# The attention stage of a vision tower on Trainium2, taken in pairs of tiles, with outputs token by token

## The reference

```python
x    = layernorm(h)
q, k = elu(x @ Wq) + 1, elu(x @ Wk) + 1          # per head, 64 channels
v    = x @ Wv
A    = (q @ k.T) * causal                         # 37 x 37, per image and head
out  = (A @ v) / max(A.sum(-1), 1e-6)
h    = h + sigmoid(x @ Wg) * (out.reshape(-1, 256) @ Wo)
```

## Time and profile before

| | |
|---|---|
| Runs (median of 3) | 1119.67 us (1112.85 to 1121.09) |
| The profiled execution's own time | 1121.94 us |
| Its span, first to last instruction | 1120.0 us |
| Mean granted clock of TensorE | 0.840 of 2.4 GHz |
| PE busy | 951.7 us (85%) |
| DVE busy | 528.6 us (47%) |

### The profile page before, as it was taken

One profiled execution on the slowest core, in us unless ns is written; L12 is line 12 of the kernel. 1 busy time (PEld: TensorE's weight loads), 2 busy tenths in 40 slices (PEclk: granted clock), 3 DMA queues, 4 the chain that ended last, 5 costly groups with the idle time before them and its releaser, 6 DMA issues.

```text
span 1120.0 us, 18357 instructions
## 1 busy us (share of the span) xinstructions
PE 951.7 (85%) x5804; PEld 664.2 (59%) x5804; DVE 528.6 (47%) x1712; ACT 323.8 (29%) x908; POOL 312.6 (28%) x308
## 2 busy tenths in 40 slices
PE   6667999968999998887769899996575999999990
PEld 5555777746664555554545467774563777777670
DVE  5983678864443232222753368864672222222210
ACT  1332233323343322222122256662201222222210
POOL 3881000000000000000042045541017277677444
PEclk9995899975557999999975579996556999999995
DMA  8778000000002999995350000000205244544222
GB/s 253 218 271 346 1 0 0 0 1 1 1 1 80 419 423 422 422 424 215 104 141 1 0 1 2 0 2 8 60 3 140 53 83 82 83 80 74 35 22 21
DMA packets 64187, 125.82 MB, mean 112 GB/s; under 512 B 26910, under 2 KB 47184, under 8 KB 54912
## 3 DMA queue, kind: packets, MB, share of 16 engines
q1 hardware_dynamic: 34176, 115.69, 28.8%
q0 software_dynamic: 29952, 9.36, 6.4%
HBM read 112.83 MB, written 11.98 MB: 111 GB/s over the span
## 4 chain that ended last, share of the span: by engine, by line
PE 67%; DMA 12%; DVE 9%; issue 6%; POOL 2%; ACT 2%; SPq 1%; DVEq 0%; POOLq 0%; ACTq 0%
PE bank L1747 14%; DMA ys<-eo 10%; PE bank L1757 6%; PE bank L738 4%; PE bank L743 3%; PE bank L1432 3%; PE bank L909 2%; PE bank L1518 2%; PE bank L1048 2%; PE bank L927 2%; PE bank L1442 2%; PE bank L1458 2%; PE bank L774 1%; PE bank L907 1%; PE bank L925 1%
## 5 line engine op out<-in xcount | busy, mean ns | idle before, releaser
L1747 PE MATMUL bank<-zT,w 96*128 96x372 f32 x512 | 161.8, 477 | 0.0
L1156 POOL MEMSET xg<- 96x74 f32 x1 | 0.2, 157 | 478.0 <-PE bank L1130 478.0
L1747 PEld LDWEIGHTS bank<-zT,w 96*128 96x128 f32 x512 | 97.4, 191 | 61.0 <-issue 0.5
L1692 POOL DMA_INDIRECT out_dram<-yr,put x48 | 105.7, 2203 | 90.0 <-issue 62.0
L1803 DVE TENSOR_TENSOR hT<-sg,bank 128x372 f32<-128x372 f32 x64 | 34.7, 542 | 126.4 <-PE bank L1747 126.4
L1678 POOL DMA_INDIRECT zr<-z_rows,take x48 | 66.5, 1385 | 85.4 <-issue 83.9
L990 DVE COPY eh<-bank 128x384 f32<-128x384 f32 x32 | 17.8, 558 | 119.4 <-PE bank L1026 119.4
L1048 PE MATMUL bank<-w2s,eg 128*64 128x192 f32 x768 | 69.4, 330 | 0.0
L1776 ACT ACTIVATE sg<-bank 128x372 f32<-128x372 f32 x64 | 30.7, 480 | 128.0 <-PE bank L1747 128.0
L715 PE MATMUL bank<-wtok_g,xT 128*111 128x192 f32 x264 | 47.9, 332 | 20.9 <-DVE y L628 20.9
L1757 PE MATMUL bank<-w2r,hT 128*124 128x192 f32 x384 | 63.7, 326 | 0.0
(11 more groups left out here) (277 smaller groups left out, 1801.0 us busy)
## 6 DMA issues: line engine op xcount, KB each, us to landing
w1s<-in_w_dram SPq DMA_DIRECT2D x32, 1152.0 KB, 12.6
w2s<-in_w_dram SPq DMA_DIRECT2D x32, 1152.0 KB, 14.7
xt<-in_x_dram SPq DMA_DIRECT2D x22, 336.0 KB, 3.9
xT<-in_xT_dram SPq DMA_DIRECT2D x22, 333.0 KB, 3.6
w<-in_w_dram SPq DMA_DIRECT2D x8, 768.0 KB
ys<-eo SPq DMA_DIRECT2D x64, 48.0 KB, 9.3
w2r<-in_w2r_dram SPq DMA_DIRECT2D x8, 384.0 KB
e<-ys SPq DMA_DIRECT2D x21, 96.0 KB, 2.0
```

Of the source, the lines that this page charges most:

```text
L1692: nc.gpsimd.indirect_dma_start(rows_out, bass.IndirectOffsetOnAxis(ap=put[:, k:k + 1], axis=0), yr[e % 2][:, j, :], None, bounds_check=OUT ...
L1747: last = nc.tensor.matmul(bank[2 + 2 * (m % 2) + part][:, 0:HS], w13[b][:, c, at:at + 128], zT[b][:, c, half * HS:(half + 1) * HS], start= ...
```

## The change

The attention stage is taken in 11 pairs of tiles, 222 tokens (`PAIR`), and each engine's program is written out in full, without the loop:

- `products_qk` moves the 222 tokens of a pair against the same 128 columns of weights: eight matmuls a pair instead of sixteen. `products_vg` is as before, twice, and is a step of its own.
- `scores`, `project` and `transpose_h` have the same matmuls, those of two tiles in one step.
- `values` holds the masked scores of a head (111 columns) and moves `vx`, which has 64 channels and a 65th column of ones: the product comes out token by token, and its 65th column is the denominator. The matmuls with ones are gone, and so is the use of half the array's columns.
- `normalize_out` bounds and inverts 4 numbers a token instead of 222 columns, and multiplies into `on`. `transpose_o` turns `on` by four transposes a pair, and ACT copies them to `oT` (`copy_oT`).
- All of `fe`, `fr`, `qk`, `vx`, `am`, `on`, `oT` and `rg` have one buffer; `ha`, `haT` and `gate` have two. Bank 7 holds, in turn, the first tile's values, the turned outputs and the projection; bank 0 the transposed input and the second tile's values.

Its core:

```diff
-                for j in range(4):
-                    for c in range(2):
-                        last = nc.tensor.matmul(bank[1][:, j * TP:(j + 1) * TP], wqk[:, c, j * 128:(j + 1) * 128], hnT[b][:, c, :], start=(c == 0), stop=(c == 1))
+                for j in range(4):
+                    for c in range(2):
+                        last = nc.tensor.matmul(bank[1 + j // 2][:, j % 2 * PAIR:(j % 2 + 1) * PAIR], wqk[:, c, j * 128:(j + 1) * 128], x[:, c, :], start=(c == 0), stop=(c == 1))
...
-                for j in range(2):
-                    for r in range(2):
-                        half = slice(64 * r, 64 * r + 64)
-                        nc.tensor.matmul(bank[5][half, j * TP:(j + 1) * TP], vx[b][:, 2 * j + r, :], am[b][:, 2 * r + j, :], start=True, stop=True)
-                for r in range(2):
-                    last = nc.tensor.matmul(bank[6][64 * r:64 * r + 64, 0:2 * TP], ones[0:TP, 0:64], am[b][:, 2 * r:2 * r + 2, :].rearrange("p j q -> p (j q)"), start=True, stop=True)
+                for i in range(2):
+                    for n in range(NH):
+                        last = nc.tensor.matmul(bank[0 if i else 7][0:TP, n * (DH + 1):(n + 1) * (DH + 1)], am[:, n % 2, i, n // 2, :], vx[:, i, n, :], start=True, stop=True)
                 last.then_inc(s_bav, 1)
...
+            def transpose_o(p):
+                pe.wait_ge(s_bon, p + 1)
+                flat = on[:].rearrange("p i h d -> p i (h d)")
+                for i in range(2):
+                    for j in range(2):
+                        last = nc.tensor.transpose(bank[7][:, (2 * i + j) * TP:(2 * i + j + 1) * TP], flat[:, i, j * 128:(j + 1) * 128], ident[0:TP, 0:TP])
+                last.then_inc(s_bt, 1)
+
+            for p in range(T // 2 + 2):
+                if p < T // 2:
+                    transpose_h(p)
+                if 1 <= p <= T // 2:
+                    scores(p - 1)
+                if p >= 2:
+                    project(p - 2)
+                if p < T // 2:
+                    products_qk(p)
+                if 1 <= p <= T // 2:
+                    values(p - 1)
+                if p < T // 2:
+                    products_vg(p)
+                if 1 <= p <= T // 2:
+                    transpose_o(p - 1)
...
+            def normalize_out(p):
+
+                dve.wait_ge(s_bav, p + 1)
+                if p:
+                    dve.wait_ge(s_bt, p)
+                out = [bank[b][0:TP, 0:NH * (DH + 1)].rearrange("p (h d) -> p h d", h=NH) for b in (7, 0)]
+                for i in range(2):
+                    last = nc.vector.tensor_scalar(den[:, i, :], out[i][:, :, DH], 1e-6, None, ALU.max)
+                last.then_inc(s_bd, 1)
+                dve.wait_ge(s_bd, 2 * p + 1)
+                nc.vector.reciprocal(rden[:], den[:]).then_inc(s_bd, 1)
+                dve.wait_ge(s_bd, 2 * p + 2)
+                for i in range(2):
+                    last = nc.vector.tensor_tensor(on[:, i], out[i][:, :, 0:DH], rden[:, i, :].unsqueeze(2).to_broadcast([TP, NH, DH]), ALU.mult)
+                last.then_inc(s_bon, 1)
```

More of the change, by code:

```diff
@@ L448, in tower @@
         s_bwo = sem("attn_projected")
+        s_bt = sem("attn_out_transposed")
+        s_bo = sem("attn_oT_copied")
         s_brg = sem("attn_gated")
@@ L538, in attention_act @@
             h_std(act, 0)
[L540 to L562, removed]
+            def copy_hT(p):
+                act.wait_ge(s_hTr, 2 * p + 2)
+                if p >= 2:
+                    act.wait_ge(s_bvg, p - 1)
+                nc.scalar.copy(haT[p % 2][:], bank[0][0:HALF, 0:2 * PAIR].rearrange("p (c q) -> p c q", c=2)).then_inc(s_hTc, 2)
@@ L564, in embed_act, with copy_oT @@
+            def copy_oT(p):
+                act.wait_ge(s_bt, p + 1)
+                if p:
+                    act.wait_ge(s_bwo, p)
+                nc.scalar.copy(oT[:], bank[7][:, 0:4 * TP].rearrange("p (i j q) -> p i j q", i=2, j=2)).then_inc(s_bo, 1)
+            for p in range(T // 2 + 1):
+                if p < T // 2:
+                    copy_hT(p)
+                    features(p)
+                    values(p)
+                if p:
+                    copy_oT(p - 1)
         def embed_act(act):
@@ L669, in mask @@
[L669 to L674, removed]
-                last.then_inc(s_bam, 1)
[L677 to L686, removed]
@@ L731, in products, with scores @@
[L731 to L735, removed]
+                    for i in range(2):
+                        last = nc.tensor.transpose(bank[0][0:HALF, c * PAIR + i * TP:c * PAIR + (i + 1) * TP], ha[p % 2][:, i, c * HALF:(c + 1) * HALF], ident[0:TP, 0:TP])
+                last.then_inc(s_hTr, 2)
+            def scores(p):
+                pe.wait_ge(s_bq, p + 1)
+                if p:
+                    pe.wait_ge(s_bam, p)
+                for i in range(2):
+                    at = slice(i * TP, (i + 1) * TP)
+                    for j in range(2):
+                        for r in range(2):
+                            rows = slice(64 * r, 64 * r + 64)
+                            last = nc.tensor.matmul(bank[5 + r][0:TP, (2 * i + j) * TP:(2 * i + j + 1) * TP], qk[rows, 2 + j, at], qk[rows, j, at], start=True, stop=True)
+                last.then_inc(s_bs, 1)
@@ new lines, in project, with products_qk @@
+            def project(p):
+                pe.wait_ge(s_bo, p + 1)
+                for i in range(2):
+                    for j in range(2):
+                        last = nc.tensor.matmul(bank[7][0:TP, i * ED:(i + 1) * ED], oT[:, i, j, :], wo[:, j, :], start=(j == 0), stop=(j == 1))
+                last.then_inc(s_bwo, 1)
+            def products_qk(p):
+                pe.wait_ge(s_hTc, 2 * p + 2)
+                if p:
+                    pe.wait_ge(s_bf, p)
+                x = haT[p % 2]
```

151 lines of the change are left out of this document (91 added, 60 removed).

## The result

The changed kernel takes 1100.77 us (median of 4 runs, 1098.82 to 1102.81), against 1119.33 for the kernel before, measured anew beside it (4 runs, 1112.85 to 1121.09): a ratio of 0.9845 with a 95% interval of 0.980 to 0.989, 18.6 us less. The profiled execution took 1102.81 us, with a span of 1101.0, 19.0 shorter than before.

A forecast was written before the change was run, and what follows sets the result against it. TensorE's queue was taken to bound the attention stage: -11.3 us of its work, +1.5 of stall and -7.4 from the clock made -17.2, so 1104.7 for the profiled execution and 1103 predicted, range 1094 to 1115.

The forecast's parts named there:

- q and k: Attention's q/k product: 3.74 us a pair become 16 records of 222 columns, 2.99, plus one exposed weight load: -0.65.
- scores: Attention scores: changing to half the rows and back happens once a pair of tiles, 0.95 us a pair, -0.2.
- projection: Attention's output projection: eight records at 0.162 us, 1.30 a pair, as the change to half the columns goes: -0.19.
- inputs: Input transposes of attention: four at 0.093 us and one start of 0.1, 0.47 a pair: -0.19.
- values: Attention values and denominators: 1.82 us a pair become 16 records, taken as 1.55: -0.27, bounds -0.95 and +0.05.
- outputs turned: New output transposes in attention: four a pair with 128 columns held, +0.47 us, bounds 0.37 and 0.66.
- The stall: PE waiting on the ACT and DVE chain in attention: 0.15 us a pair for ten pairs, +1.5, bounds 0 and +5.
- The clock: At attention's beginning the clock rises by about 104 us instead of 120: -7.4 us, bounds 0 and 9.
- The late rise (1): Rival: the clock in the attention stage rises no sooner than before, 1110 us; chance 0.15.
- a chain that binds (2): Rival: attention's single-buffered chain over ACT and DVE becomes the bound, ten pairs lose 8 us, 1111; chance 0.13.
- The third: Rival: attention's clock stays low well beyond 120 us; gain gone at 141, 1135 us if at 175; chance 0.05.
- The fourth: Rival: attention's steps cost otherwise than priced, for instance the values: -7.5 to +3.5 us; no separate chance given.

The follow-up runs named there:

- run 4: The changed kernel with each matmul of the values issued twice: 1117.78 us, +17.0 against the changed kernel.
- run 5: The changed kernel with one unused copy of 384 columns more on VectorE each pair, between features and output normalisation: 1103.53 us, +2.8.
- run 9: The kernel of run 6 with three unused products of ones in TensorE's wait behind each v product: 1132.39 us.
- Run 1: The kernel before with ten unused products of ones between the embedding and the attention stage: 1109.48 us, ratio 0.995.
- run 2: The changed kernel with ten unused products of ones ahead of the attention stage: 1100.32 us, 0.5 less than without them.
- run 3: The changed kernel with q and k in sixteen matmuls of 111 columns a pair instead of eight of 222: 1110.04 us, 9.3 more.
- run 6: The changed kernel's pairs with values, sums by ones matmuls and long reciprocal as before, outputs not turned: 1152.54 us, +51.8.
- run 8: The kernel of run 7 with further unused products of ones in TensorE's waits of the dispatch stage's first five turns: 1062.58 us.
- run 7: The changed kernel with unused products of ones ahead of attention, in waits at its end and ahead of the dispatch stage: 1096.29 us.

## Why the prediction was right

**What bounds the stage.** TensorE's queue, as read: doubling one step's records cost 1.51 us a turn of their 1.56 (run 4).

**The terms of the turn.** The forecast had 10.85 us a pair, and 10.84 was measured. By step, forecast and measured: q and k 3.09 and 3.01; v 3.02 and 3.05; scores 0.95 and 0.97; projection 1.30 and 1.39; inputs 0.47 and 0.51; values 1.55 and 1.52; outputs turned 0.47 and 0.39. The errors are small and go both ways. The one price without a row, the values', came from transposes with 111 held columns and was right. That of the turned outputs was 0.02 a record too high, since I took it from L738, which holds as many columns but is no transpose. The loss of the column tiling, by which the rule of the Trainium skill (TensorEngine Tiling, When to Use Tiling) would have made the total 2.3 us worse, isn't seen: the values cost 0.76 us a tile against 0.91 for values and sums before, where doubling L764's 0.44 would have given 0.88.

**The stall.** I took 0.15 us a pair and found none to speak of: the chain was at the lower end of its bounds, and a little under it: `on` is ready 165.45 - 161.12 = 4.33 us behind the q/k product, where I had 4.45 to 4.95. The step was rightly called critical. An operation of 0.27 us more in it costs 2.8 us (run 5), and the long reciprocal in its place would have cost 31.6 (run 9).

**The clock.** That it would rise sooner held, and the size was too small: the clock rose at 99.2 us, not by 104, and it is worth about 9 us of the stage's 20.6, where I had 7.4. The 9 are what is left of 20.6 behind eleven times 1.04, with the differences of filling and draining in them; 120 - 99.2 us at 0.46 would be 9.6. Run 1 shows the same in the kernel before, 13.1 us for the whole of its slow beginning, and runs 1 and 2 together put TensorE's work at 10.8. The reason that I gave for it, a stretch in which moving columns leave no gap, is at most a part: in run 3, with 111 columns a record, the rise came at 106.3, later but still well ahead of 120. The argument that no stretch before had 12 us without a gap doesn't hold of PE's busy time, which had none from 92.3 to 120 there. That the bet on the clock came out is in this part luck.

**The sum.** -11.3, +1.5 and -7.4 became -11.4, 0 and -9.2 at the stage's end, with the last `rg` at 220.88 where I had about 224.5. Some 1.8 us of it were lost again in later stages, which I had at nothing; without that loss the forecast would have been off by more. It hit closer than its parts. It also stands against a median of the kernel before's upper level.

**The rivals.** The late rise (1) and a chain that binds (2) didn't come, though run 6 shows that the second was one long operation away. The third, a clock that stays low, is real as well. It came about in run 6, which has fewer transposes, with a wait of 3 us in each turn, and cost 20 us. The fourth, other prices, stayed within 0.1 us a step. The Trainium skill's rule that transposes don't count as busy for the clock (TensorE: Matmul & The Clock Gate, Part 4) can't be judged from these runs, since the eight transposes of a turn always lay beside long products. The rise that the prediction held against it, at 857.3 us before, came 1 us into the product L1747 (from 856.30) and doesn't settle it either.

## What to carry to other kernels

The fp32 products of this kernel were paid by their moving columns (0.377 us a record for 448, 0.188 for 222) or, where few move, at a price that goes with the held ones (0.112 for 128, 0.096 for 111); transposes with 128 held columns were cheaper, 0.097. Before cutting steps, see which of the two each shape pays, and move more columns against the same weights where the weights are dear. Where engines hand work over with single buffers, add up the chain from one product to the next and compare it with what TensorE has to do meanwhile, for its slack is not shown by any share of busy time. And look at what TensorE does ahead of a stage and in its first turns, because a stage that can hold the full clock may not be able to win it: here 7 products of ones in the first five turns, on top of 21 ahead of them, were worth 34 us, more than the whole change.

## What was not expected

- Products of ones in waits, 28 in all, took the changed kernel from 1100.8 to 1062.6 us. The dispatch stage ran at 2.4 GHz to its last 4 us in run 8, and at 1.2 GHz for all of its 99 us in the changed kernel. In run 7 it started at the full clock too, and lost it after 3 us.
- Between kernels that differ only ahead of it, the clock's fall at the end of the attention stage and its return behind the dispatch stage hardly moved against the work: low for 116 us in both, before and after.
- A transpose with 128 held and 111 moving columns takes 0.097 us (L829, 0.39 for four) and an fp32 record of the same shape 0.112 (run 3).
- DVE's reciprocal took 2.93 us for 444 columns and 1.54 for 222, but 0.20 for 8. Next to a product over the same columns (0.62) it is by far the dearest of its operations, and with outputs token by token it is nearly gone, at 0.05 us a tile of TensorE's time (0.76 for the values and 0.20 for turning, against 0.91).
